# A two-layer convolution kernel: the shifted copy of x made on the chip, the first load moved and split, transposes without copies, shorter norms

## The reference

```python
x = x + L0(_gn(x))        # _gn: mean and variance of each channel of each image (32 groups of 1 channel)
x = x + L1(_gn(x))

# L0: depthwise 3x3, then three 32x32 channel mixes
dw  = conv(x, depthwise_weights, groups=32)
out = softmax(global) @ pointwise @ softmax(attention) @ dw

# L1: offsets from a 3x3 convolution, bilinear sampling at the shifted places, then a 3x3 convolution
off    = conv(x, w_off)               # 2 offsets per channel and pixel
mapped = bilinear(x, grid + off)      # four gathered values, two interpolations
out    = conv(mapped, w_conv) + b_conv
```

## Time and profile before

| what | value |
|---|---|
| median of 3 runs | 717.24 us |
| profiled execution | 718.9 us |
| its span | 717.1 us |
| PE busy | 684.6 us, 95% |
| DVE, ACT, POOL busy | 73%, 65%, 67% |
| queue of SP (q1) | 103.12 MB, 68.6% of the 16 DMA engines' span |
| queue of ScalarE (q10) | 11.78 MB, 9.2% |
| HBM read, written | 31.59 MB, 16.78 MB |

### The profile page before, as it was taken

One profiled execution on the slowest core, in us unless ns is written; L12 is line 12 of the kernel. 1 busy time (PEld: TensorE's weight loads), 2 busy tenths in 40 slices (PEclk: granted clock), 3 DMA queues, 4 the chain that ended last, 5 costly groups with the idle time before them and its releaser, 6 DMA issues.

```text
span 717.1 us, 10746 instructions
## 1 busy us (share of the span) xinstructions
PE 684.6 (95%) x3500; PEld 244.4 (34%) x3500; DVE 522.7 (73%) x1033; ACT 467.9 (65%) x812; POOL 478.1 (67%) x414
## 2 busy tenths in 40 slices
PE   4799979999999799999999999999999999999985
PEld 4333333333333233333333333333333333333322
DVE  3687988779956568677876589657984685578882
ACT  7587776686667365677556755576656775577870
POOL 5004867888597656866867765887658668788770
PEclk9999999999999899999999999999999999999998
DMA  8958926889557998799949896598947625477556
GB/s 142 187 111 144 143 57 158 179 178 196 126 141 165 189 213 204 171 209 189 203 112 233 173 209 152 138 236 171 225 112 177 154 66 139 114 170 178 123 118 147
DMA packets 140189, 115.64 MB, mean 161 GB/s; under 512 B 15168, under 2 KB 114016, under 8 KB 140128
## 3 DMA queue, kind: packets, MB, share of 16 engines
q1 hardware_dynamic: 116096, 103.12, 68.6%
q10 hardware_dynamic: 24032, 11.78, 9.2%
HBM read 31.59 MB, written 16.78 MB: 67 GB/s over the span
## 4 chain that ended last, share of the span: by engine, by line
PE 55%; SPq 5%; DVE 5%; ACT 3%; POOL 3%; issue 2%; DMA 1%; DVEq 0%; POOLq 0%; ACTq 0%
PE off_ps L794 27%; PE c_ps L683 24%; PE c_ps L694 2%; PE c_ps L698 2%; SPq L476 2%; SPq L395 1%; DVE other_row L1436 1%; SPq L427 1%; ACT other_row L988 1%; DMA x1b<-x1a 1%; ACT off_abs L1001 1%; DVE x1a L1421 1%; POOL row_diff L1213 1%; ACT down_ps L999 1%; POOL row_diff L1215 1%
## 5 line engine op out<-in xcount | busy, mean ns | idle before, releaser
L1436 DVE COPY_PREDICATED other_row<-down_ps,row_diff 128x768 f32<-128x768 int32 x128 | 124.7, 1028 | 124.2 <-ACT down_ps L999 124.0
L794 PE MATMUL off_ps<-x1a,wo 128*64 128x512 f32 x768 | 179.4, 601 | 4.3 <-DMA x1b<-x1a 3.7
L794 PE MATMUL off_ps<-x1b,wo 128*64 128x512 f32 x768 | 176.4, 592 | 0.0
L683 PE MATMUL c_ps<-xb,w 128*64 128x512 f32 x336 | 149.6, 593 | 2.2 <-DVE x1a L1421 1.6
L683 PE MATMUL c_ps<-mapb,w 128*64 128x512 f32 x336 | 150.8, 594 | 0.5 <-ACT bias L977 0.3
L685 PE MATMUL c_ps<-xa,w 128*64 128x512 f32 x336 | 149.6, 593 | 0.0
L988 ACT ACTIVATE other_row<-row_diff 128x768 f32<-128x768 f32 x128 | 100.7, 835 | 66.4 <-POOL row_diff L1215 43.8
L1230 POOL TENSOR_TENSOR other_row<-other_row,x_strips 128x512 f32<-128x512 f32 x48 | 57.2, 1191 | 119.1 <-DVE other_row L1448 119.0
L685 PE MATMUL c_ps<-mapa,w 128*64 128x512 f32 x294 | 131.7, 594 | 0.0
L999 ACT ACTIVATE down_ps<-off_ps,bias_o 128x512 f32<-128x512 f32 x64 | 42.0, 656 | 106.8 <-PE off_ps L794 99.4
L1231 POOL TENSOR_TENSOR other_col<-other_col,other_row 128x512 f32<-128x512 f32 x64 | 86.3, 1349 | 31.3 <-DVE other_row L1448 31.3
(11 more groups left out here) (135 smaller groups left out, 978.5 us busy)
## 6 DMA issues: line engine op xcount, KB each, us to landing
mapa<-mapped SPq DMA_DIRECT2D x224, 65.0 KB, 2.0
x1b<-x1a SPq DMA_DIRECT2D x28, 520.0 KB, 6.5
mapb<-mapa SPq DMA_DIRECT2D x28, 520.0 KB, 7.6
out_dram<-x1a SPq DMA_DIRECT2D x49, 256.0 KB, 4.7
xb<-in_x_dram SPq DMA_DIRECT2D x48, 256.0 KB, 9.9
xa<-in_x_dram ACTq DMA_DIRECT2D x40, 256.0 KB, 8.7
x_strips<-x1a SPq DMA_DIRECT2D x112, 81.2 KB, 2.5
x_strips<-x1a SPq DMA_DIRECT2D x112, 65.0 KB, 2.5
```

The costliest lines, as they stand in the source:

```text
L683: nc.tensor.matmul(bank[0:64, :], weights[:, kx, :], rows_b[:, of, kx:kx + W], start=(kx == 0), stop=(kx == 2))
L794: last = nc.tensor.matmul(off_ps[k % 2][64 * t:64 * t + 64, CH * n:CH * n + CH], wo[wpar][:, kx, side:side + 2 * C], rows[:, b:b + 7:2, kx ...
L1436: last = dve.copy_predicated(other_row[n][:, :, KR // 2 * odd:KR // 2 * odd + KR // 2, :], bass.AP(tensor=rows.tensor, offset=rows.offset ...
```

## The change

- Image 0's load goes first in SP's stream, in three parts (16, 12 and 4 blocks) with a semaphore each. The small weights move to ScalarE's queue.
- `xb` of images 1 to 7 is no longer loaded from DRAM with 8 transfers, but copied from `xa` with 4 (64 partitions by 2080 elements, pads included). Each copy waits for its half of `xa`. In SP's stream the second half's copy now stands behind the strip moves of the next image.
- The L1 weights are transposed straight from where they were loaded: 36 matmuls of 32 output rows, read with a step of 9 elements, in front of and between the three small products. ScalarE's eight copies go.
- VectorE takes the three small results from PSUM between the statistics of image 0, one after each of the groups 0, 1 and 2.
- `w1_base` is two GpSimd operations with broadcast operands in place of 18.
- `norm` aggregates the four row parts at once (one operation in place of a statistics, a sum, an aggregate and a scaling), and the Newton steps are five operations in place of six. `w1` is scaled in two operations that no longer wait for each other.

```diff
+        FIRST_PARTS = [(0, HB), (HB, BL - 4), (BL - 4, BL)]
+        first_loaded = [xa_loaded[0], xa_loaded[1], rest_loaded]
 ...
         @block.sync
         def _(sp):
-            sp.dma_start(soft_in[:, 0, :], att_w).then_inc(soft_load, DMA)
-            sp.dma_start(soft_in[:, 1, :], glob_w).then_inc(soft_load, DMA)
-            sp.dma_start(pw_sb, pw_w.rearrange("o c a b -> o (c a b)")).then_inc(l0_load, DMA)
+            for part in range(3):
+                load_first(sp, part)
 ...
-                for q in range(4):
-                    first = b + 1 if q < 2 else b
-                    sp.dma_start(to[Q * q:Q * q + Q, first:first + HB, 1:W + 1], rows[:, b:e, (q + 2) % 4, :])\
-                      .then_inc(loaded[half], DMA)
+                for first, p, p_from in ((b + 1, 0, 2 * Q), (b, 2 * Q, 0)):
+                    sp.dma_start(to[p:p + 2 * Q, first:first + HB, :].rearrange("p b w -> p (b w)"),
+                                 rows[p_from:p_from + 2 * Q, b:e, :].rearrange("p b w -> p (b w)"))\
+                      .then_inc(copied[half], DMA)
 ...
                 if after and prev:
-                    for half in range(2):
-
-                        sp.wait_ge(conv1_done, 8 * (i + 1) + (5 if half == 0 else 8))
-                        load_xb(i + 2, half, xb_loaded)
+                    sp.wait_ge(conv1_done, 8 * (i + 1) + 5)
+                    sp.wait_ge(xa_loaded[0], xa_count(i + 2))
+                    copy_xb(i + 2, 0, xb_copied)
 ...
-                    for half in range(2 if i >= 2 else 1):
-                        move_strips(sp, i + 1, half)
+                    move_strips(sp, i + 1, 0)
+                    if prev and after:
+                        sp.wait_ge(conv1_done, 8 * (i + 1) + 8)
+                        sp.wait_ge(xa_loaded[1], xa_count(i + 2))
+                        copy_xb(i + 2, 1, xb_copied)
+                    if i >= 2:
+                        move_strips(sp, i + 1, 1)
 ...
         def _(pe):
             pe.wait_ge(s_setup["pool"], 2)
+            pe.wait_ge(l1_load, 2 * DMA)
+            def transpose_taps(to, weights, n, ky):
+                of = weights.rearrange("p (c t) -> p t c", t=TAPS)
+                for rp in range(2):
+                    j = rp + ky
+                    for t in range(3 * ky, 3 * ky + 3):
+                        last = nc.tensor.matmul(to[Q * j:Q * j + Q, n * t:n * t + n], of[:, t, :], ident[0:n, 0:n],
+                                                start=True, stop=True)
+                return last
 ...
-            act.wait_ge(l1_load, 2 * DMA)
-            for r in range(4):
-                act.activation(off_rep[:, :, r, :], w_off_sb.rearrange("p (c t) -> p t c", t=TAPS), ACT.Copy)
-                last = act.activation(conv_rep[:, :, r, :], w_conv_sb.rearrange("p (c t) -> p t c", t=TAPS), ACT.Copy)
 ...
-                step(dve.bn_stats(four_stats[:, :], four_mv[:, 0, :]))
-                step(dve.reduce_sum(var_sum[:, :], four_mv[:, 1, :], AX))
-                settle(apart=True)
-                step(dve.bn_aggr(mv[:, :], four_stats[:, :]))
-                step(dve.tensor_scalar(var_sum[:, :], var_sum[:, :], 0.125, 0.5 * EPS, ALU.mult, ALU.add))
-                settle()
-                step(dve.tensor_scalar(mv[:, 1:2], mv[:, 1:2], 0.5, var_sum[:, :], ALU.mult, ALU.add))
+                step(dve.bn_aggr(mv[:, :], four_mv[:, :, :]))
+                settle()
+                step(dve.tensor_scalar(mv[:, 1:2], mv[:, 1:2], 0.5 * ROOT, 0.5 * ROOT * EPS, ALU.mult, ALU.add))
 ...
+            def first_stats():
+                for (b, e), loaded in zip(FIRST_PARTS, first_loaded):
+                    dve.wait_ge(loaded, LOADS * DMA)
+                    for g in range(b // 4, e // 4):
+                        group_stats(0, g)
+                        if g < 3:
+                            mix_step(g)
```

More of the change, by code:

```diff
@@ L503, in copy_mapb @@
                 copy_rows(mapb, mapa, 4 * half, 4, mapb_copied[half])
-            for half in range(2):
-                load_x(sp, 0, half, xa_loaded)
-            for half in range(2):
-                sp.wait_ge(xa_loaded[half], LOADS * DMA)
+            for loaded in first_loaded:
+                sp.wait_ge(loaded, LOADS * DMA)
             for half in range(2):
@@ L655, in _ @@
             pe.wait_ge(s_setup["pool"], 2)
+            pe.wait_ge(l1_load, 2 * DMA)
[7 more added lines that the diff above has]
+                return last
+            for ky in range(3):
+                transpose_taps(off_ps[0], w_off_sb, 2 * C, ky)
             pe.wait_ge(s_setup["dve"], 2)
@@ L658, in _ @@
               .then_inc(s_setup["pe"], 1)
+            transpose_taps(down_ps, w_conv_sb, C, 0)
             pe.wait_ge(s_setup["dve"], 3)
-            pe.wait_ge(l0_load, 5 * DMA)
+            pe.wait_ge(pw_load, DMA)
             nc.tensor.matmul(c_ps[1][0:32, 0:32], pw_sb, glob_t, start=True, stop=True).then_inc(s_setup["pe"], 1)
+            transpose_taps(down_ps, w_conv_sb, C, 1)
             pe.wait_ge(s_setup["dve"], 4)
             nc.tensor.matmul(c_ps[2][:, 0:32], att_rep, pg, start=True, stop=True).then_inc(s_setup["pe"], 1)
[L665 to L674, removed]
+            transpose_taps(down_ps, w_conv_sb, C, 2).then_inc(s_setup["pe"], 1)
             def conv_group(bank, weights, rows_b, rows_a, g, first_done, is_spread=False):
@@ L1174, in _ @@
             pool.wait_ge(s_setup["dve"], 5)
[L1175 removed]
+            pool.wait_ge(l0_load, 4 * DMA)
             pool.wait_ge(s_setup["pool"], 3)
@@ L1178, in _ @@
             for rp in range(2):
-                for ky in range(3):
-                    j = rp + ky
-                    p = slice(Q * j, Q * j + Q)
-                    for kx in range(3):
-                        last = pool.tensor_scalar(w1_base[p, kx, C * rp:C * rp + C], mix_t[p, :],
-                                                  dw_sb[p, 3 * ky + kx:3 * ky + kx + 1], None, ALU.mult)
+                taps = dw_sb[:, 3 - 3 * rp:6 - 3 * rp].unsqueeze(2).broadcast_to([P, 3, C])
+                last = pool.tensor_tensor(w1_base[:, :, C * rp:C * rp + C], mix_t.unsqueeze(1).broadcast_to([P, 3, C]),
+                                          taps, ALU.mult)
             last.then_inc(s_setup["pool"], 1)
@@ L1372, in x_stats @@
                     dve.wait_ge(xa_loaded[half], xa_count(i))
-                rows = xa_of(i)
                 for g in range(NG // 2 * half, NG // 2 * (half + 1)):
-                    step(dve.bn_stats(stats_x[:, g, :], rows[:, 4 * g:4 * g + 4, 1:W + 1]))
+                    group_stats(i, g)
+            def first_stats():
+                for (b, e), loaded in zip(FIRST_PARTS, first_loaded):
+                    dve.wait_ge(loaded, LOADS * DMA)
[3 more added lines that the diff above has]
+                            mix_step(g)
             def x_norm(i, par):
@@ L1454, in bank @@
                 return c_ps[place[job] % 3]
-            for half in range(2):
-                x_stats(0, half)
+            first_stats()
             dve.wait_ge(s_setup["pool"], 2)
```

116 lines of the change are left out of this document (65 added, 51 removed).

## The result

The changed kernel takes 728.98 us (median of 4 runs, 725.96 to 732.4), against 722.24 us for the kernel before in the same comparison (4 runs, 716.29 to 728.07). Two of these four (727.23 and 728.07 us) are executions in a slower state, and the ratio leaves them out: it compares with the 716.8 us of the other two. It is 1.0172, with a 95% interval of 1.009 to 1.0253. So the changed kernel is slower by 1.7%: the interval leaves out 1 and takes in 2%. I had predicted 708.5 us and at most 715.5. The profiled execution took 725.96 us, with a span of 724.2 us; before it was 717.1.

What follows compares the result with a forecast made beforehand. TensorE was taken as the bound, with only its idle time and slow stretches to win. Gains of 3.2 + 0.8 + 5.5 = 9.5 us gave 708.5 us; forecast 705 to 711 (chance 0.55), range 703.5 to 715.5.

Steps and rivals of the forecast that it cites:

- The start: Image 0's load to the first `w1` matmul: 2.4 us from earlier statistics plus 0.8 from the norm, 3.2 us.
- The norm: Statistics to the first `w1` matmul: fewer operations make it 0.8 us shorter.
- The second wait: TensorE's 3.8 us wait for the pads of image 2's `xb`: 0.8 us shorter, with the clock still falling.
- The third wait: TensorE's 3.7 us wait for image 2's `x1b`: gone with its 3.0 us clock cost, less 1.2 for `mapb`: 5.5 us.
- The later images: Images 3 to 7: SP's pauses absorb the new wait for `xa`, and copies move as many bytes: zero.
- given back later: Rival, chance 0.08: SP stops for image 2's late `xa` loads, up to 4 us come back, 712 to 713 us.
- what I said would show me wrong: A wait for `xb` or `mapb` of over 3 us, or a longer stretch from 250 to 620 us.

Runs made afterwards that it cites:

- e7: The kernel before with only the shorter norms and the two-part scaling of `w1`; 717.9 us, ratio 0.9988.
- e3: The changed kernel with `xb` loaded from DRAM at the places of the copies, without the waits for `xa`; 717.98 us, ratio 0.998.
- e1: The changed kernel with `xb` loaded from DRAM again, at the places of the kernel before; 722.83 us, ratio 1.0055.
- e11: The changed kernel, copies included, with both halves of the store issued by ScalarE in place of SP; 713.91 us, ratio 0.9942.
- e9: The changed kernel with its `xb` copies in rows of 512 bytes in place of pieces of 8320; 734.01 us, ratio 1.0195.
- e4: The changed kernel with the `xb` copies of images 3 to 7 issued by ScalarE in place of SP; 733.73 us, ratio 1.0203.
- e10: e3 with both halves of the store issued by ScalarE in place of SP; 710.78 us, ratio 0.9874.

## Why the prediction was wrong

- **The start** (forecast 3.2 us sooner with the norm; 2.24 at the first matmul, 1.33 at chunk (0, 0)). The weights were there at 8.73 us and not at 5.0: the small loads on ScalarE's queue landed late beside the image's load, that of `w_conv` 6.3 us after its issue where it had been 2.2. The transposes cost little: 36 passes in 2.79 us, 0.078 us each, and twelve in 0.69, 0.058 each, where I had taken 0.10 and bounded by 0.054 and 0.217. Against the 0.054 that I had estimated without the step, these are 1.4 and 1.1 times as much, where I had reckoned 1.8 from ScalarE's rows. The third product was out of PSUM at 13.58 us and five statistics stood behind it, as said. The 0.9 us that are lost behind the first matmul are slow passes: in the first group those of 512 columns took 1.06 us nearly to its end and then 0.59, and it was 5.4 us up to the second group, in before 4.5. A pass takes 1.06 us also where the granted clock is 0.50 (508 to 510 us), but the profile has 1.00 from 21 to 28 us, so it is not shown that this is the clock. Over the kernels that share this start, chunk (0, 0) lay between 0.67 and 2.94 us ahead, so one profile doesn't fix it.
- **The norm** was right: 16.80 to 21.41 us is 4.6 in place of 5.5, and e7 by itself 0.89 sooner, against 0.8.
- **The second wait** went from 3.8 to 3.5 us, and the lead grew by 0.1 us there where I had said 0.8. The clock fell in it as I had assumed: the granted clock was 0.50 from 103 to 105 us before and from 102 to 105 us in the changed kernel.
- **The third wait** gave 2.5 us where I had said 5.5. `x1b` was issued at 233.12 us, 2.9 us sooner than before. TensorE came there 1.4 us sooner as well, so SP gained 1.4 us on it where I had said 4.5, and 2.3 us of the wait stayed. The clock fell all the same, where I had counted on a wait without a fall: it was 0.50 from 242 to 244 us, and in before it had been 0.50 from 242 to 248. For SP's way to the store I had reckoned 1.4 us for `x1b`, 13 for the strips, 1.4 for the second pair and 10.1 for the 16 moves to `mapa`. The term that failed is the last: right behind the second pair of copies the moves took 13.0, and 10.03 behind the loads of e3. The strips took 13.4 us. No run shows what the 13 of the forecast rests on. What the runs show in its place are single issues behind `x1b`: of the 14.98 us of before in the earlier trace rows, the first two moves took 2.18 and 2.60 us and the sixth 1.88, the others 0.59 or 0.60; in the changed kernel the first two took 1.93 and 2.32, another 0.80 and the others 0.59 or 0.60.
- **The later images** are the step that failed. I said "I count zero" because SP had pauses and the copy moves as many bytes. They cost 11.4 us in the profile. Two parts of that step were wrong. One is the copy that costs what the load did: the bytes are the same, but behind each second pair of copies SP's next two issues took some 3 us longer than behind e3's loads (1.9 us of it net at image 1). For image 4 the first pair came out of its pause as well, since the wait for `xa` held it to 250.89 us. The other is that a lead is kept: SP's stream had no slack for it, and e1, with `xb` loaded as before, gave back 10.5 us. Both ended in the same two waits, for the store and for `mapb`, and with the stores out of the stream (e11) they are nearly gone. The rival "given back later" named the right wait, for `mapb` of image 2, with a price of up to 4 us and a chance of 0.08. It saw one of its three places, did not see ScalarE's wait for the store, and reckoned SP's stream to get earlier with TensorE. That stream had hardly a pause from 250.9 to 324.7 us and did not: the last `mapb` went out 3.5 us later than before.
- The sign of what I said would show me wrong held: a wait of over 3 us for `mapb`, and a longer stretch from 250 to 620 us.

What stays open, besides the split between the gap and the copies: why e1 loses another 5 us from image 5 on (its chunk starts go from -1.7 to +3.7) and e3 does not. In e1's profile the same two waits return there, ScalarE's for the store (10.5 and 10.4 us) and TensorE's for `mapb` (2.1 and 1.3 us), but no run tells why its stream is that late then.

## What to carry to other kernels

Before a load is replaced by a copy of the same bytes, look at the issues right behind it: equal bytes did not mean equal time of the queue here. Before a transfer is made to wait for something, look where its bytes will move then, and what small, ordered transfers stand behind them. A lead of the busiest engine is kept only if the streams that feed it have slack further on; so find the next transfers that it will wait for and their issue times in the trace, for each later round and not for the first, and test the theory by taking work out of that stream.

## What the runs showed of the hardware

- Small loads on ScalarE's queue took two to three times as long to land when the image's loads went out on SP's from 0.75 us on, and not from 2.13: 5.2 us in the changed kernel and 2.3 before for 72 KB, 6.3 and 2.2 us for 36 KB.
- Small moves of 65 to 81 KB were mostly issued in 0.59 us each. Right behind two copies of 520 KB inside SBUF the next two issues took 1.8 to 2.5 us (changed kernel, images 1 to 5). Behind four loads of 256 KB from DRAM at the same place they took 0.5 to 0.6 us in all but one of ten cases (e3, the one 1.93 us). Rows of 512 bytes in place of pieces of 8320 didn't help (e9: three issues of 1.1 to 2.7 us).
- SP's issues were slow beside copies on ScalarE's queue too: in e4, from 270.5 us on, when ScalarE issued its copies for image 4, moves to `x_strips` took up to 2.6 us each, and 0.59 us just before.
- When the stores moved to ScalarE's queue (e10), the moves to `mapa` beside them went from 0.63 and 0.76 us each on the mean (e3) to 0.89 and 0.87.
